# Lane numbers and the second scan's result in a PSUM bank, and a transpose that waits for one-hots

## What is computed

```
hi = x[src] @ w1;  hj = x[tgt] @ w2
e = leaky_relu(hi + hj, 0.3) * a
logits = e.reshape(-1, HEAD, OUT_CH).sum(-1)
seg_max = segment_max(logits, tgt)
exp = exp(logits - seg_max[tgt])
attn = exp / segment_sum(exp, tgt)[tgt]
out = segment_sum(hi.reshape(-1, HEAD, OUT_CH) * attn[:, :, None], tgt)
x = layernorm(x + out)
ef = (relu(edge_attr @ We1 + be1) @ We2 + be2) * sigmoid(ts @ Wt + bt)
msg = relu(concat(x[row], ef) @ Wn1 + bn1) @ Wn2 + bn2
x = layernorm(x + segment_sum(msg, col) + x)
```

## Time and profile before

| what | value |
|---|---|
| device time, three runs | 3327.63, 3344.86, 3351.23 us; median 3344.86 |
| span of the profiled execution, first to last instruction | 2205.4 us |
| its busy time: PE, DVE, ACT, POOL | 1817.9, 1325.7, 658.7, 1607.1 us |
| granted TensorE clock, mean over the span | 0.892 |
| first phase's gathers (L707) | 831, from 31.7 to 1088.8 us |
| second phase's gathers (L741) | 831, first one in the tail at 1145.9 us |

### The profile page before, as it was taken

One profiled execution on the slowest core, in us unless ns is written; L12 is line 12 of the kernel. 1 busy time (PEld: TensorE's weight loads), 2 busy tenths in 40 slices (PEclk: granted clock), 3 DMA queues, 4 the chain that ended last, 5 costly groups with the idle time before them and its releaser, 6 DMA issues.

```text
span 2205.4 us, 47181 instructions
## 1 busy us (share of the span) xinstructions
PE 1817.9 (82%) x12720; PEld 1413.0 (64%) x12721; DVE 1325.7 (60%) x3725; ACT 658.7 (30%) x1410; POOL 1607.1 (73%) x1701
## 2 busy tenths in 40 slices
PE   6778888888887788888879888888888888788887
PEld 6455666666665566666657667666766676667665
DVE  6454667565665666656645456666566666665665
ACT  6111112111121111111114344444444444444432
POOL 5777777777777777777517777777777777777775
PEclk9897879888799989888869999999999999899898
DMA  8722333333333333333245444444444444444441
GB/s 233 153 82 84 82 85 102 89 95 85 94 96 84 95 88 96 92 87 95 60 135 154 129 135 127 141 127 142 134 134 128 140 127 141 126 142 130 137 126 45
DMA packets 239385, 252.30 MB, mean 114 GB/s; under 512 B 141011, under 2 KB 187720, under 8 KB 239315
## 3 DMA queue, kind: packets, MB, share of 16 engines
q1 hardware_dynamic: 185036, 141.15, 21.5%
q0 software_dynamic: 54000, 110.28, 19.4%
q10 hardware_dynamic: 288, 0.13, 0.0%
HBM read 233.20 MB, written 13.22 MB: 112 GB/s over the span
## 4 chain that ended last, share of the span: by engine, by line
POOL 51%; issue 21%; PE 15%; DVE 5%; DMA 4%; DVEq 1%; POOLq 1%; ACT 1%; SPq 0%; ACTq 0%
POOL T L741 31%; POOL G L707 20%; PE ps L1854 3%; PE ps L1831 2%; DMA G<-hi_rows,idx 2%; PE ps L1826 2%; PE ps L1858 2%; PE ps L1787 1%; PE ps L2069 1%; DVEq L1316 1%; DVE msg L1336 1%; PE ps L2060 1%; DMA T<-y_rows,idx 1%; PE ps L2075 0%; ACT V L895 0%
## 5 line engine op out<-in xcount | busy, mean ns | idle before, releaser
L741 POOL DMA_INDIRECT T<-y_rows,idx x831 | 788.0, 948 | 310.2 <-issue 249.4
L707 POOL DMA_INDIRECT G<-hi_rows,idx x831 | 804.1, 968 | 263.3 <-issue 248.4
L2060 PE MATMUL ps<-G 128*128 128x64 f32 x1664 | 227.3, 283 | 117.5 <-DVE acc L1613 116.9
L999 ACT ACTIVATE G<-G 128x512 f32<-128x512 f32 x208 | 131.0, 630 | 582.4 <-DVE G L1619 582.4
L2060 PEld LDWEIGHTS ps<-G 128*128 128x128 f32 x1664 | 216.0, 203 | 129.4 <-issue 128.9
L1826 PE MATMUL ps<-ident,G 128*128 128x128 f32 x828 | 151.1, 312 | 161.7 <-issue 81.0
L1619 DVE TENSOR_TENSOR G<-ps,T 128x512 f32<-128x512 f32 x208 | 143.6, 690 | 225.9 <-DMA T<-y_rows,idx 217.4
L2069 PE MATMUL ps<-wN,G 128*128 128x128 f32 x1664 | 253.3, 300 | 28.5 <-DVE T L1578 28.4
L895 ACT ACTIVATE V<-ps 128x512 f32<-128x512 f32 x207 | 123.6, 597 | 464.3 <-PE ps L1831 463.8
L1854 PEld LDWEIGHTS ps<-oh,msg 128*128 128x128 f32 x1608 | 236.0, 222 | 33.2 <-issue 24.0
L1854 PE MATMUL ps<-oh,msg 128*128 128x64 f32 x1608 | 251.0, 307 | 1.4 <-DVE mX L1413 0.8
(11 more groups left out here) (238 smaller groups left out, 2263.6 us busy)
## 6 DMA issues: line engine op xcount, KB each, us to landing
T<-in_edge_weight SPq DMA_DIRECT2D x103, 512.0 KB
Dbc<-block_destinations SPq DMA_DIRECT2D x69, 384.0 KB
T<-in_edge_attr SPq DMA_DIRECT2D x103, 256.0 KB
G<-hi_rows,idx POOLq DMA_INDIRECT x831
T<-y_rows,idx POOLq DMA_INDIRECT x831
link<-scan_destinations SPq DMA_DIRECT2D x280, 16.1 KB
hi_rows<-T SPq DMA_DIRECT2D x12, 256.0 KB, 4.4
mX<-in_x SPq DMA_DIRECT2D x15, 192.0 KB
```

The source lines that it names most:

```text
L707: pool.indirect_dma_start(out=G[:, s, t * C:(t + 1) * C], out_offset=None, in_=hi_d[:, :], in_offset=bass.IndirectOffsetOnAxis(ap=idx[:, s ...
L741: pool.indirect_dma_start(out=Yb[:, r, t * C:(t + 1) * C], out_offset=None, in_=y_d[:, :], in_offset=bass.IndirectOffsetOnAxis(ap=idx[:, r ...
L2060: ins = pe.matmul(sums_of(g4), hS[i][:, n * C:(n + 1) * C], ohB[i][:, n * W:(n + 1) * W], start=(n == 0), stop=(n == 3))
```

## The change

Two new views lie in unused columns of the bank `EXp`: `lanes`, columns 320 to 383, and `R2p`, columns 384 to 511. The lane numbers are copied to `lanes` once, ahead of the first phase's loop, when the projections that used the bank are done. The window one-hots of the loop read `lanes` instead of `iotaF`; the second scan writes `R2p` instead of `R2`, and the third and the fourth read it. Since TensorE writes the same bank with its transpose of exponentials, that transpose now waits for the one-hots of its group. The code of the last groups keeps `iotaF` and `R2`, but for the wait in front of the transpose of group A.

```diff
+        lanes, R2p = EXp[:, 320:320 + W], EXp[:, 384:384 + P]
...
+            known = steps[0]
...
+                dve.wait_ge(s_hic, NU + 1)
+                dve.tensor_copy(lanes, iotaF[:, :]).then_inc(s_own, 1)
+                dve.wait_ge(s_own, known + 1)
...
-                        dve.tensor_tensor_scan(R2[0:BR, :], link[:, bs, 0:P], logit, shp[0:BR, 0:1], ALU.add,
+                        dve.tensor_tensor_scan(R2p[0:BR, :], link[:, bs, 0:P], logit, shp[0:BR, 0:1], ALU.add,
...
-                        dve.tensor_tensor_scan(R3[0:BR, ::-1], link[:, bs, P:0:-1], R2[0:BR, ::-1], -1e30, ALU.add,
+                        dve.tensor_tensor_scan(R3[0:BR, ::-1], link[:, bs, P:0:-1], R2p[0:BR, ::-1], -1e30, ALU.add,
...
-                        dve.tensor_tensor_scan(R4[0:BR, ::-1], link[:, bs, P:0:-1], R2[0:BR, ::-1], shp[0:BR, 1:2],
+                        dve.tensor_tensor_scan(R4[0:BR, ::-1], link[:, bs, P:0:-1], R2p[0:BR, ::-1], shp[0:BR, 1:2],
...
-                                          iotaF[:, :].unsqueeze(1).to_broadcast([P, cnt, W]),
+                                          lanes.unsqueeze(1).to_broadcast([P, cnt, W]),
...
                         pe.wait_ge(s_exp, p + 1)
+                        pe.wait_ge(s_oh, p + 1)
                         need(pe, s_msg, p)
                         pe.transpose(EXp[:, 0:BR].rearrange("p (r k h) -> p k r h", r=QR, k=QR), EXT[0:BR, :], ident[0:BR, 0:BR]).then_inc(s_ext, 1)
...
                 pe.wait_ge(s_msg, A)
+                pe.wait_ge(s_oh, A + 1)
                 turned_exp(A, EXp)
```

## The result

| | kernel before | after |
|---|---|---|
| median device time | 3348.34 us | 3366.36 us |
| ratio, 95% interval | | 1.0049 (1.0030 to 1.0069) |
| span, mean granted clock of a profiled execution | 2205.4 us, 0.892 (the one read for the prediction) | 3372.8 us, 0.748 |

A forecast was written before the change was run, and what follows sets the result against it. The prediction took POOL's gathers to bound the first phase. Its terms, -17.5 for freed gathers, +1.5 for new alignments and +0.9 in the tail, summed to -15.1 us, from 3344.9 to 3329.8 us, range 3306 to 3349.

The forecast's parts named there:

- What bounds the kernel: First phase: said to be as long as POOL's gathers, 831 at one per 1.248 us, with TensorE and VectorE following.
- 1139.5 above the span, and I take that part as unchanged: Median of the runs, 3344.86 us, less the traced span of 2205.4, taken as constant time outside the span.
- Gathers freed, -17.5: First phase: gathers no longer held by one-hots, third and fourth scan once these read PSUM, -17.5 us.
- L1290's new alignments, +1.5: First phase: new alignment of POOL and VectorE may put more gathers on the 128x512 one-hots, 0 to 3.1 us, taken as 1.5.
- Durations of the edited operations, 0: One-hots and scans on VectorE: their own durations unchanged with PSUM operands, and VectorE works behind POOL, 0 us.
- The wait in the steady phase, 0: TensorE's transpose of exponentials: one-hots end before it anyway, by 0.22 us at the tightest and 0.83 at the median, 0 us.
- The rival "slower": TensorE stands behind the one-hots in each step; a 33 us loss needs one-hots of 3.0 us; time 3378; chance 0.05.
- The tail, +0.9: Tail: the wait binds once, as the transpose of 1098.88 waits for one-hots that end at 1100.93, +0.9 us.
- forecast's own range: Total time if the forecast, a gain of 8 to 33 us with chance 0.68, holds: 3315 to 3340 us.

The follow-up runs named there:

- e17: Kernel before with the first phase's indirect gathers all using one column of row numbers 0 to 127, chip E: 2198.71 us, ratio 0.9995.
- e16: The change as a whole once more, against the kernel before on chip E: 2187.08 us, ratio 0.9948.
- e1: Kernel before plus only the change's two waits of TensorE's transposes for the one-hots, chip A: 3365.5 us, ratio 1.0033.
- e8: Kernel before plus only the two waits of TensorE's transposes for the one-hots, again, chip C: 3367.36 us, ratio 1.0086.
- e2: Kernel before with only the second scan's result R2 in PSUM, no new wait, lanes in SBUF: 3355.1 us, ratio 1.0007.
- e4: Kernel before with every second gather of the first phase left out, chip B: 2840.08 us, ratio 0.8752.
- e7: Kernel before with a group's gathers also waiting for all three aggregates of the group four back: 3318.65 us, ratio 1.0227.
- e9: Kernel before with the first phase's indirect gathers replaced by plain DMAs of the same size from GpSimd, chip C: 2486.27 us, ratio 0.7441.
- e10: Kernel before with the first phase's gathers replaced by plain DMAs from SyncE's queue, chip C: 2603.56 us, ratio 0.7792.
- e12: Kernel before with the first phase's indirect gathers all using one column of row numbers 0 to 127, chip D: 2200.63 us, ratio 1.0009.
- e5: Kernel before with each group's one-hots made in two instructions, eight of twelve blocks early, chip B: 3238.36 us, ratio 0.9955.

## Why the prediction was wrong

- **What bounds the kernel** failed. "So POOL never waits for a free buffer" holds for the first trace alone. In the timed executions POOL waits 703 us for the messages, and TensorE's late updates set the period, 26 us instead of 15.2.
- **"1139.5 above the span, and I take that part as unchanged"** is the step at which it could have been seen. Around the span lie 2.1 us. On chip A the difference is 731.5 in the first phase (1788.6 against 1057.1) and 393.3 in the second (1452.8 against 1059.5). A time half as long again as the span was the loudest number shown, and it was put aside as a constant.
- **Gathers freed, -17.5.** Right for executions like the traced one (-16.6 by busy time against the first trace, 804.1 to 787.5, and -14.1 against e17 on one chip). In the timed ones the term is 0: the gathers last 945 ns in before as in after. They start only when the messages are done, so they no longer meet the one-hots.
- **L1290's new alignments, +1.5.** Near 0: the gathers that met it were stretched by 1.4 us in e16 and, by the same count, by 1.5 in the first trace. In all, the sum leaves 21.3 - 17.5 + 1.5 = 5.3 us over 0.942 us a gather; on chip E 787.5 less 831 x 0.942 is 4.7.
- **Durations of the edited operations, 0.** Right: one-hots 955 ns against 958 in the earlier trace rows, second scan 471 against 463, third 421 against 425. The Trainium skill (Perfetto Trace Analysis, Optimizing Scalar/DVE Operations) gives some 60 ns of overhead on SBUF and 125 on PSUM; the 65 ns between them show in none of these three.
- **The wait in the steady phase, 0.** Mis-sized for the timed executions: in the first phase of one execution each it measures +16 us on chip A (e1) and +17.1 on chip C (e8), by the ratios 11 and 29, and it is the whole result. The margin of 0.22 to 0.83 us was read from a trace in which the third aggregate ended at 8.1 us; at 18.3 us the order of transpose and one-hots is the other way round in half of the groups.
- **The rival "slower"** had the right mechanism and the wrong price and trigger. It asked for one-hots of 3.0 us. They still take 0.96; it is what they wait for that came 10 us later. It named no such cause and so got 0.05.
- **The tail, +0.9,** can't be told from the scatter of these runs.
- **A slip:** a gain of 8 to 33 us from 3344.9 is 3312 to 3337, not the "forecast's own range" of 3315 to 3340.

Shown: the waits make the loss (e1, e8 against e2), on three chips late updates go with indirect gathers in flight (e4, e7, e9, e10), and the change gains where no update is late (e16). Open: why the indirect gathers do this on three chips and not on two, and whether the recording of the executions has a part in it; whether it is the indirect form or the scattered rows (e12 and e17 both fell on chips where nothing is late); and why the waits cost 73 us beside the early one-hots on chip B, where the waits alone were not run. Of what ran there, the early one-hots (e5) are the best complete kernel on chip B, 0.9955, and the change is the best on chip E, 0.9948. No version here was shown to gain on both kinds.

## What to carry to other kernels

Hold the traced execution's time against the timed ones before anything else: where they disagree by more than a few per cent, the trace's bound and margins are those of another regime, and the range must cover both. A new wait is free only by the margin of the execution that is timed; a margin that hangs on an update coming in time should be priced again with that update late. And where one queue issues long runs of indirect gathers, look for engines that idle on "remote" beside them, and ask for fewer gathers before tuning the work around them.

## What the runs showed of the hardware

- Of five chips, the same program took 2198 and 2200 us on two and 3247, 3341 and 3350 on three. With plain DMAs in the first phase that phase took 928 us on a chip of the first kind and 932 on one of the second.
- On the second kind, the semaphore updates of TensorE's aggregates came 7.5 to 7.6 us late on average from 1.25 us behind the start of a group's first indirect gather on, and 0.03 to 0.04 us with none in flight; in the stretch shown the granted clock was 1.00. The third aggregate's came mostly 2.5 to 3.2 us behind the last gather's end. Halving the gathers cut the mean to 2.86 (e4); plain DMAs of the same bytes, from GpSimd or SyncE, to 0.01 (e9, e10).
- On chip E, where GpSimd sets the pace, a gather that VectorE's 128x768 comparison met 0.13 us behind its start was stretched in 29 of 38 cases with both inputs in SBUF (e17) and in none of 49 with one in PSUM (e16).
